# An attention and mixture-of-experts layer on one core: a prologue with real transposes, a stacked low-rank matmul, and V of batch 1 moved between the row maxima

## The chip, the cores and the metric

The kernel runs on one core of a Trainium2 chip. The metric is the device time of one execution in microseconds. The core has TensorE (PE; its weight loads are shown as PEld), VectorE (DVE), ScalarE (ACT), GpSimd (POOL) and SyncE (SP). Each runs its own list of instructions strictly in the order written, and they wait for one another by semaphores. SP and POOL also issue the DMAs here.

## The reference

The input x has 2 batches of 1024 tokens of 512 numbers, all float32. One post-norm layer is computed:

```python
def lora_linear(x, W, b, Bm, Am):                       # rank 16, SCALING = 0.5
    out = jnp.einsum('bld,od->blo', x, W) + b
    upd = jnp.einsum('blr,or->blo', jnp.einsum('bld,rd->blr', x, Bm), Am)
    return out + SCALING * upd
q, k, v = (_split(lora_linear(x, W, b, B, A)) for ...)  # 16 heads of 32
attn = jax.nn.softmax(jnp.einsum('bhqd,bhkd->bhqk', q, k) * SCALE, axis=-1)
out = jnp.einsum('bhqk,bhkd->bhqd', attn, v)            # back to (B, L, 512)
x = _layernorm(x + lora_linear(out, Wo, bo, Bo, Ao))
# 8 experts, hidden 704, top-1 routing with capacity 256, and a shared expert
x = _layernorm(x + moe(x, Wg, W1, W3, W2) + shared(x, sw1, sw3, sw2))
```

The low-rank update is folded into the weights: the kernel forms the transpose of W + 0.5 * Am Bm once for each of q, k, v and the output projection, and then needs a single matmul with it.

## The kernel before

**Two-part numbers.** Nearly every matmul runs in float32r (type FR). An operand is kept as a rounded high part, which ScalarE writes, and a low part (the rest), which VectorE writes by a subtraction. A product is three matmuls: high x high, high x low, low x high (`SPLIT`, `split3`, L712 to L718). So whatever comes out of TensorE into a PSUM bank and serves as an operand later goes through ScalarE and then through VectorE. There are 8 banks of 128 x 512.

**The prologue** is the part in front of the first attention half, and the only part that the change touches, but for three waits.

1. The four A matrices of the low-rank terms are transposed (L734) and copied by ScalarE, scaled by 0.5, to `lora_at` (L1114).
2. `weights(n)` makes one folded weight, in the order `W_ORDER` = v, q, k, output. Each has four chunks of 128 x 512. A chunk is a float32 matmul over 16 rows (the low-rank term, L747) and four float32 matmuls with the identity on top of it (the transpose of W, L750). Two banks alternate (`w_bank`). The parts of v stay in SBUF (`wv`); those of the others go through two staging buffers (`w_stage`) and by POOL's DMAs to DRAM (`wt_d`, L615), and a staging buffer is filled again when its store has landed (L1121, L1357).
3. x is loaded in 16 tiles of 128 tokens through four buffers (`xin`), transposed by TensorE (`turn_x`, L723) and split into `xT` (L1109, L1347).
4. `make_v` computes V for a token tile by 12 matmuls of 128 x 512 (L716), VectorE adds the bias (L1369) and POOL stores it to DRAM (`v_d`, L620), through two buffers `v_sb`.
5. TensorE's order of these is: weights(0) = v, x tiles 0 to 3, weights(1) = q, V 0 to 3, x 4 to 7, weights(2) = k, V 4 to 7, x 8 to 11, V 8 to 11, x 12 to 15, V 12 to 15.
6. Four projection units (12 matmuls each, L794) give k and q of batch 0 for the first four heads, with one chunk of the output weights behind each. ScalarE and VectorE split them into planes (L1145, L1388), and SP copies the planes into the stacked operands `Qs` and `Ks` (L420), 96 rows for each head.
7. The softmax needs the maximum of each score row. `PRO_USES` lists 44 score tiles (TensorE L806, VectorE's row maximum L1398) and one `mrow`, a transpose of the 16 columns of negated maxima (L810), stored by VectorE (L1402) and copied by SP to row 96 of `Qs` (L427). These go through three banks (`WORK`). `PRO_PLACE` puts three more projection units, for batch 1, as whole blocks behind score tiles 10, 18 and 26.
8. POOL, when all stores have landed and all of x is split, writes row 96 of both `Ks` with ones (L634).

Then attention runs in 16 halves (4 groups of 4 heads, 2 batches, 2 halves of 512 queries). A half computes transposed scores (L843), exponentials on ScalarE (L1172) into `prob`, and the product with V (L856). Between them, by the written orders `EVEN` and `ODD`, come the next halves' score tiles for the maxima and quarters of projection units. The first L843 marks the end of the prologue. The SBUF memory of `prob`, `Qs[1]` and `Ks[1]` is the same as that of the prologue's buffers, so ScalarE waits for all of the prologue's stores before its first exponential.

Of the kernel before, what the change touches and what calls it, by code (L numbers as in the profile page):

```python
# [51 lines left out]
W_ORDER = (2, 0, 1, 3)  # L52
# [70 lines left out]
PRO_USES = smax_uses(1) + [("mrow",)] + smax_uses(2, 0, EARLY[0])  # L123
PRO_PLACE = [10, 18, 26]
# [105 lines left out]
def emit(nc, ctx, x, W, bias, bo, Bm, Am, Wg, W1, W3, W2, sw1, sw3, sw2, out):  # L230
# [56 lines left out]
    xin = [stp(f"xin{i}", [P, D], F32) for i in range(4)]  # L287
    w_stage = [[stp(f"w_stage{i}{s}", [P, D], FR) for s in ("hi", "lo")] for i in range(2)]
# [82 lines left out]
    def _(sp):  # L371
# [14 lines left out]
        def load_x(i):  # L386
            for j in range(4):
                if i:
                    sp.wait_ge(sem("x_t"), 4 * i + j - 3)
                sp.dma_start(xin[j][:], x_rows[(4 * i + j) * P:(4 * i + j + 1) * P, :]).then_inc(sem(f"x_ld{j}"), 16)  # L390
# [63 lines left out]
        for i in range(2):  # L454
            for s in range(2):
                sp.wait_ge(sem(f"w_st{i}_{s}"), 16 * 6)

        def half(v):
            if v.proj and v.slot % 2 == 0:
# [4 lines left out]
                if not v.first:  # L464
                    sp.wait_ge(sem("pv_done"), used)
# [24 lines left out]
        def load_wo(v):  # L490

            sp.wait_ge(sem("st_full"), v.halves(HG * KC))
            for s in range(2):
                sp.dma_start(f32(wo[s][:]), wt_d[3, s]).then_inc(sem("wo_ld"), 16)
# [104 lines left out]
    def _(po):  # L599
# [9 lines left out]
        def store_w(n):  # L609
            m = W_ORDER[n]  # L610
            for dc in range(DC):
                k = (n - 1) * DC + dc
                po.wait_ge(sem("w_lo"), k + DC + 1)
                for s in range(2):
                    po.dma_start(wt_d[m, s][:, dc, :], f32(w_stage[k % 2][s][:])).then_inc(sem(f"w_st{k % 2}_{s}"), 16)  # L615

        def store_v(i):
            for t in range(4 * i, 4 * i + 4):
                po.wait_ge(sem("v_done"), t + 1)
                po.dma_start(v_d[t * P:(t + 1) * P, :], v_sb[t % 2][:]).then_inc(sem(f"v_st{t % 2}"), 16)  # L620

        store_w(1)
        store_v(0)
        store_w(2)
        for i in range(1, 4):
            store_v(i)
        store_w(3)
        for i in range(2):
            for s in range(2):
                po.wait_ge(sem(f"w_st{i}_{s}"), 16 * 6)  # L630
            po.wait_ge(sem(f"v_st{i}"), 16 * NT // 2)
        po.wait_ge(sem("x_lo"), NT)
        for i in range(2):
            po.memset(f32(Ks[i][96:97, :, :]), 1.0).then_inc(sem("ks_ones"), 1)  # L634
# [76 lines left out]
    def _(pe):  # L711
# [19 lines left out]
        pe.wait_ge(sem("lora_ld"), 16 * 8)  # L731
# [974 lines left out]
```

## Time and profile before

| | |
|---|---|
| median of 3 runs | 1193.78 us (1190.91, 1193.78, 1624.03) |
| the profiled execution | 1192.78 us |
| its span | 1191.2 us |
| mean granted TensorE clock | 0.954 |
| TensorE busy | 1126.8 us, 95% of the span, 5834 matmuls |
| VectorE busy | 722.0 us, 61% |
| ScalarE busy | 552.0 us, 46% |
| GpSimd busy | 482.7 us, 41% |
| DMA | 136.58 MB, 115 GB/s mean |

The span is cut by the program into pieces in which an engine is busy. A granted clock of 1.00 means TensorE's full 2.4 GHz, 0.50 means 1.2 GHz, and numbers between are means over a stretch. At the lower level every matmul takes twice as long and so TensorE shows as busy for twice as long; its busy share alone tells little. In the rows by stretch the columns are the stretch, its length, then busy time (and instructions) of PE, PEld, DVE, ACT and POOL, the granted clock, the share of the DMA engines and GB/s. A row of the chain of waits gives the start, the length, the engine and the line. In the rows in order of time a bracket gives the idle time of the engine in front of the group, and what ended it; "x11" means eleven instructions, and a float32 matmul over 128 rows or 16 rows shows as two. Where no bracket stands the engine hadn't been idle.

### The profile page before, as it was taken

To read this page: it belongs to the slowest core of one execution; us is meant where nothing else is said; L and a number is where in the kernel's file an instruction comes from. 1 tells how busy PE (TensorE), PEld (TensorE's weight loads), DVE (VectorE), ACT (ScalarE), POOL (GpSimd) and SP (SyncE) were. 2 spreads that over 40 slices of the span, in tenths; PEclk is the share of its full clock that TensorE was granted. 3 is DMA by queue.
4 is the path that set the end of the run, shared out by engine and by line. 5 is a ranking of instruction groups with operands and counts; after the bars stand their busy time and mean duration, and the time that the engine had idled before them with its cause. 6 is when DMAs were issued, how large, how long until landed. Compare 5 with 4: busy or idle time off the path is not lost.

```text
span 1191.2 us, 16459 instructions
## 1 busy us (share of the span) xinstructions
PE 1126.8 (95%) x5834; PEld 768.8 (65%) x5834; DVE 722.0 (61%) x1194; ACT 552.0 (46%) x960; POOL 482.7 (41%) x290
## 2 busy tenths in 40 slices
PE   7999689999999999999999979895999999999995
PEld 4687454656555564646543457674789999998774
DVE  1332476787877777777885468351356666664153
ACT  2211016565656656565666522331246666664125
POOL 0311207778584848587786731055000000002500
PEclk7999669999999999999999989897999999999997
DMA  4663415040332324140438253061147776765603
GB/s 155 221 207 110 120 28 134 25 98 30 76 94 63 81 58 120 37 107 21 99 85 230 60 173 106 18 207 23 53 116 220 203 226 198 233 192 119 100 1 141
DMA packets 151686, 136.58 MB, mean 115 GB/s; under 512 B 43121, under 2 KB 119153, under 8 KB 151360
## 3 DMA queue, kind: packets, MB, share of 16 engines
q1 hardware_dynamic: 143040, 113.45, 34.6%
q0 software_dynamic: 8576, 22.23, 6.5%
q8 instruction: 41, 0.67, 0.2%
q14 instruction: 29, 0.24, 0.1%
HBM read 79.72 MB, written 31.47 MB: 93 GB/s over the span
## 4 chain that ended last, share of the span: by engine, by line
PE 88%; DVE 5%; issue 2%; ACT 2%; DMA 1%; SPq 1%; POOL 0%; ACTq 0%; DVEq 0%
PE bank L716 27%; PE bank L972 11%; PE bank L843 11%; PE bank L806 11%; PE bank L856 10%; PE bank L794 8%; PE bank L868 4%; PE bank L750 2%; PE bank L723 2%; PE bank L747 2%; DVE mx L1398 1%; ACT rows L1314 1%; DVE rows L1530 1%; DMA at_in<-attn_d 0%; DVE xTlo L1347 0%
## 5 line engine op out<-in xcount | busy, mean ns | idle before, releaser
L1398 DVE TENSOR_REDUCE mx<-bank 128x1 f32<-128x512 f32 x512 | 322.6, 680 | 114.6 <-PE bank L806 112.5
L1172 ACT ACTIVATE prob<-bank 128x512 f32<-128x512 f32 x512 | 289.7, 597 | 202.4 <-PE bank L843 189.2
L646 POOL TENSOR_TENSOR psum<-psum,prob 128x1024 f32<-128x1024 f32 x122 | 286.8, 2395 | 0.0
L843 PE MATMUL bank<-Qs,Ks 97*128 97x512 f32 x512 | 208.7, 424 | 1.0 <-ACT prob L1172 0.9
L806 PE MATMUL bank<-Ks,Qs 96*128 96x512 f32 x512 | 196.1, 431 | 11.7 <-DMA Qs<-plane_qhi 7.3
L843 PEld LDWEIGHTS bank<-Qs,Ks 97*128 97x128 f32 x512 | 96.0, 189 | 111.5 <-ACT prob L1172 74.4
L646 POOL TENSOR_TENSOR psum<-prob,prob 128x1024 f32<-128x1024 f32 x32 | 75.8, 2388 | 176.7 <-PE bank L868 133.2
L806 PEld LDWEIGHTS bank<-Ks,Qs 96*128 96x128 f32 x512 | 100.2, 197 | 60.7 <-DVE mx L1398 24.2
L856 PE MATMUL bank<-prob,V 128*32 128x512 f32 x1024 | 131.4, 601 | 0.0
L695 POOL DMA_DIRECT2D oe_d<-oe_sb x16 | 8.7, 547 | 256.4 <-ACT oe_sb L1294 255.4
L1239 ACT ACTIVATE sa<-bank 128x256 f32<-128x256 f32 (+1 forms) x72 | 32.7, 455 | 157.5 <-PE bank L716 120.4
L1516 DVE TENSOR_TENSOR sa<-bank,sa 128x256 f32<-128x256 f32 (+1 forms) x72 | 37.0, 514 | 109.0 <-ACT sa L1239 86.1
L794 PE MATMUL bank<-xThi,Wsl 128*128 128x512 f32 x256 | 101.6, 419 | 0.0
L1440 DVE RECIPROCAL bank<-bank 128x128 f32<-128x128 f32 x64 | 60.2, 951 | 14.8 <-PE bank L868 14.8
L794 PEld LDWEIGHTS bank<-xThi,Wsl 128*128 128x128 f32 x256 | 51.7, 202 | 12.5
L856 PEld LDWEIGHTS bank<-prob,V 128*32 128x32 f32 x1024 | 24.0, 108 | 51.3 <-issue 35.0
L794 PE MATMUL bank<-xTlo,Wsl 128*128 128x512 f32 x128 | 53.0, 414 | 0.0
L972 PE MATMUL bank<-w2hi,hid0hi 128*128 128x512 f32 x96 | 39.8, 415 | 9.0 <-issue 8.7
L972 PE MATMUL bank<-w2hi,hid1hi 128*128 128x512 f32 (+1 forms) x96 | 39.5, 412 | 2.8 <-DVE hid1lo L1518 2.8
L1509 DVE TENSOR_TENSOR w2lo<-raw,w2hi 128x512 fp32r<-128x512 f32 (+1 forms) x60 | 41.0, 685 | 1.9 <-ACT w2hi L1232 1.8
L681 POOL DMA_INDIRECT xd_d<-rows,sidx x16 | 17.0, 1060 | 57.1 <-DVE sidx L1580 52.6
L972 PE MATMUL bank<-w2hi,hid0lo 128*128 128x512 f32 x96 | 38.6, 402 | 0.8 <-issue 0.8
(213 smaller groups left out, 2147.5 us busy)
## 6 DMA issues: line engine op xcount, KB each, us to landing
raw<-in_L_ffn_W_dram SPq DMA_DIRECT2D x120, 256.0 KB
Ks<-plane_khi SPq DMA_DIRECT2D x64, 128.0 KB, 2.3
Qs<-plane_qhi SPq DMA_DIRECT2D x64, 128.0 KB, 2.3
raw<-in_L_ffn_sw_dram SPq DMA_DIRECT2D x30, 256.0 KB
xin<-in_L_attn_x_dram SPq DMA_DIRECT2D x16, 256.0 KB, 4.2
v_d<-v_sb POOLq DMA_DIRECT2D x16, 256.0 KB, 2.3
Wsl<-wt_d SPq DMA_DIRECT2D x16, 256.0 KB, 4.3
Ks<-plane_klo SPq DMA_DIRECT2D x32, 128.0 KB, 2.3
```

Of the source, the lines that this page charges most:

```text
L646: po.tensor_tensor(psum[:, pr], (prob[0] if kc == 1 else psum)[:, pr], prob[kc % RING][:, pr], ALU.add).then_inc(sem("sum_done"), 1)
L716: mm = nc.tensor.matmul(dst, lhs(a, dc), rhs(b, dc), start=dc == 0 and k == 0, stop=dc == DC - 1 and k == 2)
L794: mm = nc.tensor.matmul(pj, Wsl[:, m, a, dc, :], xT[p][:, dc, cols], start=dc == 0 and k == 0, stop=dc == DC - 1 and k == 2)
L806: mm = nc.tensor.matmul(dst, Qs[b][0:96, hh, q0:q0 + P], Ks[b][0:96, hh, part * 512:part * 512 + 512], start=True, stop=True)
L843: nc.tensor.matmul(score_at(v, i), Ks[v.b][0:97, hh, kc * P:(kc + 1) * P], Qs[v.b][0:97, hh, v.hf * HALF:(v.hf + 1) * HALF], start=True, s ...
L856: mm = nc.tensor.matmul(ov[hh * HD:(hh + 1) * HD, :], V[b][:, kc % KC, hh * HD:(hh + 1) * HD], prob[kc % RING][:, hh, :], start=kc == 0, s ...
L868: mm = nc.tensor.matmul(dn[hh * HD:(hh + 1) * HD, :], ones32[:], part[:, hh, :], start=summed[n] == 1, stop=summed[n] == KC - SUMS[n] + 1)
L972: mm = nc.tensor.matmul(bank[4 + i], hid[c % 2][a][p0:P, i * P:(i + 1) * P], w2[p][p0:P, c, :], start=c == 0 and k == 0, stop=c == FC - 1 ...
L1172: ACTV(prob[kc % RING][:, hh, :], score_at(v, i), ACT.Exp, scale=SCALE).then_inc(sem("exp_done"), 1)
L1398: ins = RED(mx[(hf + ahead) % 2][:, 4 * hh + qt, part:part + 1], src, AX.X, ALU.max)
L1440: nc.vector.reciprocal(part, part).then_inc(sem("rden"), 1)
L1509: TT(w2[1][p0:P, c], raw2[c % 2][p0:P, :], f32(w2[0][p0:P, c]), ALU.subtract).then_inc(sem("conv2"), 1)
```

## The change

- `W_ORDER` becomes q, k, v, output.
- A weight chunk is four transposes in TensorE's transpose form and then one float32r matmul over 80 rows. Its operands are `bs` and `as_`: B is loaded five times, one copy for each 16 rows (`load_b`), ScalarE rounds all 80 rows and VectorE puts the low part into rows 32 to 47; A's high part is copied by ScalarE to rows 0 and 32, and VectorE puts its low part into row 64 on; the rows between are zeroed by POOL first. The matmul so adds the three products of the split at once.
- x has eight buffers instead of four. Its last eight tiles are turned behind the four projection units.
- V is computed for tiles 0 to 3 behind the three weights, for 4 to 7 between the first four projection units, and for batch 1 (8 to 15) by quarters in a written order `PRO_ORDER`: `m` is a score tile, `r` the mrow, `v` a quarter of V, `a` VectorE's addition and POOL's store for it, `p` a quarter of a projection unit, `q` its split, `w` a chunk of the output weights, `s` its split and store.
- `mrow` comes after 36 score tiles instead of 32.
- The second `Ks` row of ones is written at the end, the first at the start. Some waits for stores move to where the data is first used.

```diff
-W_ORDER = (2, 0, 1, 3)
+W_ORDER = (0, 1, 2, 3)
+RSTACK = 80
...
-PRO_USES = smax_uses(1) + [("mrow",)] + smax_uses(2, 0, EARLY[0])
-PRO_PLACE = [10, 18, 26]
+PRO_USES = smax_uses(1) + smax_uses(2, 0, 4) + [("mrow",)] + smax_uses(2, 4, EARLY[0])
+PRO_ORDER = ("vvvv a vm vm vm vm a vm vm vm vm a vm vm vm vm a wm pm pm pm pm s vm "
+             "vmq vm vm a wm vm s vm vm vm a pm pm pm pm wm vm sq vm vm vm a wm r "
+             "s vm vm vm vm a pm pm pm pm q")
...
+    fresh = Arena(nc, small_at - V_BYTES * 2, small_at)
+    xin += [fresh(f"xin{i}", [P, D], F32) for i in range(4, 8)]
...
+    def staged(n, dc):
+
+        return (n if n < 2 else n - 1) * DC + dc
...
         for m in range(4):
-            sp.dma_start(lora_b[32 * m:32 * m + RANK, :], Bm[m]).then_inc(sem("lora_ld"), 16)
             sp.dma_start(lora_a[:, m], Am[m].rearrange("(c p) r -> p c r", p=P)).then_inc(sem("lora_ld"), 16)
+
+        def load_b(m):
+
+            for r in range(0, RSTACK, RANK):
+                sp.dma_start(lora_b[r:r + RANK, m], Bm[m]).then_inc(sem("b_ld_first" if m == 0 else "b_ld"), 16)
...
         load_w(0)
+        load_b(0)
         load_x(0)
+        for m in range(1, 4):
+            load_b(m)
         load_w(1)
-        sp.dma_start(bv_bc[:], bias[2].rearrange("(o d) -> o d", o=1).to_broadcast([P, D])).then_inc(sem("bv_ld"), 16)
         load_x(1)
         load_w(2)
+        sp.dma_start(bv_bc[:], bias[2].rearrange("(o d) -> o d", o=1).to_broadcast([P, D])).then_inc(sem("bv_ld"), 16)
+        load_w(3)
         load_x(2)
         load_x(3)
-        load_w(3)
...
-        stack_unit(0, 3, 4)
+        stack_unit(0, 2, 4)
         for i in range(2):
-            sp.wait_ge(sem(f"v_st{i}"), 16 * NT // 2)
+            sp.wait_ge(sem(f"v_st{i}"), 16 * NT // 4)
+        sp.wait_ge(sem("x_t"), NT)
         load_v(0, 0)
...
+        po.wait_ge(sem("const"), 2)
+        po.memset(f32(as_[0:RSTACK]), 0.0).then_inc(sem("as_zero"), 1)
+        po.wait_ge(sem("as_zero"), 1)
+        po.memset(f32(Ks[0][96:97, :, :]), 1.0).then_inc(sem("ks_ones"), 1)
+        for n in range(2):
             for dc in range(DC):
...
+                store_w(n, dc)
+        for t in range(2 * DC):
+            store_v(t)
+        t, dc = 2 * DC, 0
+        for w in "".join(PRO_ORDER.split()):
+            if w == "a":
+                store_v(t)
+                t += 1
+            elif w == "s":
+                store_w(3, dc)
+                dc += 1
         for i in range(2):
             for s in range(2):
                 po.wait_ge(sem(f"w_st{i}_{s}"), 16 * 6)
...
+        po.memset(f32(Ks[1][96:97, :, :]), 1.0).then_inc(sem("ks_ones"), 1)
...
-            pe.wait_ge(sem("a_ev"), n + 1)
+            pe.wait_ge(sem("a_lo"), n + 1)
+            pe.wait_ge(sem("b_lo"), 1 if n == 0 else 2)
             pe.wait_ge(sem(f"w_ld{n % 2}"), 16 * (n // 2 + 1))
...
-                nc.tensor.matmul(dst, lora_b[32 * m:32 * m + RANK, dc * P:(dc + 1) * P],
-                                 lora_at[32 * m:32 * m + RANK, :], start=True, stop=False)
                 for oc in range(DC):
-                    mm = nc.tensor.matmul(dst[:, oc * P:(oc + 1) * P], w_raw[n % 2][:, oc, dc * P:(dc + 1) * P],
-                                          ident[:], start=False, stop=oc == DC - 1)
+                    nc.tensor.matmul(dst[:, oc * P:(oc + 1) * P], w_raw[n % 2][:, oc, dc * P:(dc + 1) * P],
+                                     ident[:], start=oc == 0, stop=False, is_transpose=True)
+                mm = nc.tensor.matmul(dst, bs[0:RSTACK, m, dc * P:(dc + 1) * P], as_[0:RSTACK, m, :],
+                                      start=False, stop=True)
                 mm.then_inc(sem("w_mm"), 1)
...
+        pe.wait_ge(sem("a_lo"), 4)
         weights(0)
-        pe.wait_ge(sem("a_ev"), 4)
         turn_x(0)
         weights(1)
-        make_v(0)
         turn_x(1)
         weights(2)
-        make_v(1)
-        for i in (2, 3):
-            turn_x(i)
-            make_v(i)
+        for t in range(4):
+            make_v(t)
...
-        pe.wait_ge(sem("x_lo"), NT)
-
         for n, (m, ph) in enumerate(PRO_PROJ[:4]):
             project_unit(m, ph, 0, range(DC), n or None, 48)
-            weights(3, n, n + 1)
...
+            make_v(4 + n)
+        turn_x(2)
+        turn_x(3)
+        pe.wait_ge(sem("x_lo"), NT)
...
+        def split_a(n):
+
+            m = W_ORDER[n]
             ac.wait_ge(sem("a_t"), n + 1)
-            ACTV(lora_at[32 * m:32 * m + RANK, :], bank[n][0:RANK, :], ACT.Copy, scale=LORA).then_inc(sem("a_ev"), 1)
+            for r in (0, 32):
+                ACTV(as_[r:r + RANK, m], bank[n][0:RANK, :], ACT.Copy, scale=LORA).then_inc(sem("a_ev"), 1)
+
+        ac.wait_ge(sem("as_zero"), 1)
+        split_a(0)
+        ac.wait_ge(sem("b_ld_first"), 16 * 5)
+        ACTV(bs[0:RSTACK, 0], lora_b[0:RSTACK, 0], ACT.Identity).then_inc(sem("b_hi"), 1)
+        for n in range(1, 4):
+            split_a(n)
+        ac.wait_ge(sem("b_ld"), 16 * 15)
+        ACTV(bs[0:RSTACK, 1:4], lora_b[0:RSTACK, 1:4], ACT.Identity).then_inc(sem("b_hi"), 1)
...
+                if n != 2 and at >= 2:
+                    ac.wait_ge(sem(f"w_st{at % 2}_0"), 16 * (at // 2))
+                ACTV(wv[0][:, dc, :] if n == 2 else w_stage[at % 2][0][:], w_bank(k),
                      ACT.Identity).then_inc(sem("w_hi"), 1)
```

In the written order TensorE, ScalarE, VectorE and POOL each walk through `PRO_ORDER` and take the letters that are theirs. VectorE's part of the split of A and B:

```diff
+        def split_a(n):
+
+            m = W_ORDER[n]
+            ve.wait_ge(sem("a_ev"), 2 * n + 2)
+            nc.vector.scalar_tensor_tensor(out=as_[64:64 + RANK, m], in0=bank[n][0:RANK, :], scalar=LORA,
+                                           in1=f32(as_[0:RANK, m]), op0=ALU.mult, op1=ALU.subtract).then_inc(sem("a_lo"), 1)
+
+        def split_b(k, ms):
+
+            ve.wait_ge(sem("b_hi"), k + 1)
+            TT(bs[32:32 + RANK, ms], lora_b[32:32 + RANK, ms], f32(bs[32:32 + RANK, ms]),
+               ALU.subtract).then_inc(sem("b_lo"), 1)
```

## Rows read from the trace of the kernel before

**Rows 1.** The page's part 4, shares of the chain of waits by engine.
```profile
PE 88%; DVE 5%; issue 2%; ACT 2%; DMA 1%; SPq 1%; POOL 0%; ACTq 0%; DVEq 0%
```

**Rows 2.** Busy time by stretch: us; each engine's busy time; granted clock, DMA.
```profile
0.00:36.00 36.00, 28.77 (x113) 18.07 (x114) 6.82 (x10) 9.49 (x15) 3.27 (x12) 0.81 0.57 181
118.00:126.00 8.00, 0.73 (x7) 0.57 (x5) 0.69 (x1) 0.60 (x1) 1.35 (x3) 0.79 0.90 262
126.00:161.00 35.00, 29.93 (x68) 19.02 (x68) 21.56 (x35) 2.06 (x3) 6.67 (x2) 0.65 0.21 51
168.50:180.00 11.50, 10.93 (x38) 8.21 (x36) 9.20 (x15) 6.45 (x12) 3.87 (x2) 0.77 0.11 25
180.00:200.00 20.00, 20.00 (x112) 8.79 (x116) 13.68 (x24) 13.12 (x24) 19.62 (x9) 1.00 0.49 112
```

**Rows 3.** Chain of waits in order of time: start us, us, what.
```profile
6.57 3.56 PE bank L734 x16
27.56 1.05 PE bank L747 x2
28.61 1.09 PE bank L750 x8
36.12 11.21 PE bank L716 x48
47.33 1.75 PE bank L723 x16
60.41 11.58 PE bank L716 x48
98.87 2.81 PE bank L794 x12
168.52 0.43 PE bank L843
174.00 0.23 PE bank L843
```

**Rows 4.** SyncE's issues in order of time: start us, us, what.
```profile
3.90 0.50 SPq L378 DMA_DIRECT2D lora_b<-in_L_attn_Bo_dram  x1
4.44 0.42 SPq L379 DMA_DIRECT2D lora_a<-in_L_attn_Ao_dram  x1
```

**Rows 5.** DMA issues of the first 195 us: size, median us to landing.
```profile
w_raw<-in_L_attn_Wv_dram SPq DMA_DIRECT2D x1, 1024.0 KB, 5.7
lora_b<-in_L_attn_Bo_dram SPq DMA_DIRECT2D x1, 32.0 KB, 2.2
wt_d<-w_stage0hi POOLq DMA_DIRECT2D x6, 256.0 KB, 2.7
wt_d<-w_stage1hi POOLq DMA_DIRECT2D x6, 256.0 KB, 3.6
```

**Rows 6.** ScalarE in order of time, in brackets the idle time before.
```profile
10.15 0.58 ACT L1114 ACTIVATE lora_at<-bank 16x512 f32<-16x512 f32 x1 [0.24 <-PE bank L734]
37.12 0.60 ACT L1122 ACTIVATE w_stage0hi<-bank 128x512 fp32r<-128x512 f32 x1 [4.65 <-DMA wt_d<-w_stage0hi]
```

**Rows 7.** VectorE in order of time.
```profile
30.36 0.69 DVE L1358 TENSOR_TENSOR w_stage0lo<-bank,w_stage0hi 128x512 fp32r<-128x512 f32 x1 [1.32 <-ACT w_stage0hi L1122]
86.65 2.47 DVE L1347 TENSOR_TENSOR xTlo<-bank,xThi 128x512 fp32r<-128x512 f32 x4
117.24 0.75 DVE L1388 SCALAR_TENSOR_TENSOR plane_qlo<-bank,bcol,plane_qhi 128x512 fp32r<-128x512 f32 x1 [2.19 <-ACT plane_qhi L1145]
126.69 6.67 DVE L1398 TENSOR_REDUCE mx<-bank 128x1 f32<-128x512 f32 x11 [6.72 <-PE bank L806]
```

**Rows 8.** GpSimd in order of time.
```profile
31.38 0.77 POOL L615 DMA_DIRECT2D wt_d<-w_stage0hi  x1 [29.70 <-DVE w_stage0lo L1358]
125.72 6.95 POOL L634 MEMSET Ks<- 1x4096 f32 x2 [4.38 <-DMA wt_d<-w_stage1lo]
```

**Rows 9.** TensorE in order of time, after the gap at 118 us.
```profile
125.89 6.53 PE L806 MATMUL bank<-Ks,Qs 96*128 96x512 f32 x11 [7.27 <-DMA Qs<-plane_qhi]
```

More of the change, by code:

```diff
@@ L463, in half @@
                 c, used = value(v.g * P + (v.h // 4 * P + v.b * P)), value(v.halves(KC))
-                if not v.first:
+                if v.first:
+                    for i in range(2):
+                        sp.wait_ge(sem(f"v_st{i}"), 16 * NT // 2)
+                else:
                     sp.wait_ge(sem("pv_done"), used)
@@ L492, in load_wo @@
             sp.wait_ge(sem("st_full"), v.halves(HG * KC))
+            for i in range(2):
+                for s in range(2):
+                    sp.wait_ge(sem(f"w_st{i}_{s}"), 16 * 6)
             for s in range(2):
@@ L630, in _ @@
                 po.wait_ge(sem(f"w_st{i}_{s}"), 16 * 6)
[L631 to L634, printed above, removed]
+        po.memset(f32(Ks[1][96:97, :, :]), 1.0).then_inc(sem("ks_ones"), 1)
+        po.wait_ge(sem("ks_ones"), 2)
         def sums(n):
@@ L730, in _ @@
         pe.wait_ge(sem("const"), 2)
[L731 removed]
+        pe.wait_ge(sem("lora_ld"), 16 * 4)
         for n, m in enumerate(W_ORDER):
@@ L767, in make_v @@
                     pe.wait_ge(sem("v_done"), t - 1)
-                split3(bank[6 + t % 2], lambda a, dc: xT[a][:, dc, t * P:(t + 1) * P],
-                       lambda p, dc: wv[p][:, dc, :]).then_inc(sem("v_mm"), 1)
+            for dc in quarters:
+                for k, (a, p) in enumerate(SPLIT):
+                    mm = nc.tensor.matmul(bank[6 + t % 2], xT[a][:, dc, t * P:(t + 1) * P], wv[p][:, dc, :],
+                                          start=dc == 0 and k == 0, stop=dc == DC - 1 and k == 2)
+            if DC - 1 in quarters:
+                mm.then_inc(sem("v_mm"), 1)
+        pe.wait_ge(sem("a_lo"), 4)
         weights(0)
-        pe.wait_ge(sem("a_ev"), 4)
         turn_x(0)
         weights(1)
-        make_v(0)
         turn_x(1)
         weights(2)
-        make_v(1)
-        for i in (2, 3):
-            turn_x(i)
-            make_v(i)
+        for t in range(4):
+            make_v(t)
         def project_unit(m, ph, b, quarters, n, ld_need):
@@ L1149, in _ @@
             plane_hi(m, ph, n + 1, 48, None)
-            weights(3, n, n + 1)
+        turned_x(2)
+        turned_x(3)
+        i, dc = 4, 0
+        for w in "".join(PRO_ORDER.split()):
+            if w == "q":
+                plane_hi(*PRO_PROJ[i], i + 1, 48, 96)
+                i += 1
+            elif w == "s":
+                weights(3, dc, dc + 1)
+                dc += 1
         for i in range(2):
@@ L1362, in turned_x, with make_v @@
                 turned(i, j, bank[j], "x_hi", "x_lo")
-        def make_v(i):
-            for t in range(4 * i, 4 * i + 4):
-                ve.wait_ge(sem("v_mm"), t + 1)
-                if t >= 2:
-                    ve.wait_ge(sem(f"v_st{t % 2}"), 16 * (t // 2))
-                TT(v_sb[t % 2][:], bank[6 + t % 2], bv_bc[:], ALU.add).then_inc(sem("v_done"), 1)
+        def make_v(t):
+            ve.wait_ge(sem("v_mm"), t + 1)
+            if t >= 2:
+                ve.wait_ge(sem(f"v_st{t % 2}"), 16 * (t // 2))
+            TT(v_sb[t % 2][:], bank[6 + t % 2], bv_bc[:], ALU.add).then_inc(sem("v_done"), 1)
         weights(0)
@@ L1373, in _ @@
         weights(1)
-        ve.wait_ge(sem("bv_ld"), 16)
-        make_v(0)
         turned_x(1)
         weights(2)
-        make_v(1)
-        for i in (2, 3):
-            turned_x(i)
-            make_v(i)
+        ve.wait_ge(sem("bv_ld"), 16)
+        for t in range(4):
+            make_v(t)
         def plane_lo(m, ph, n):
@@ L1409, in _ @@
             plane_lo(m, ph, n + 1)
-            weights(3, n, n + 1)
-        for n, kind in enumerate(PRO_USES):
-            use(kind, n, n + 1, 1, None)
-            if n - 1 in PRO_PLACE:
-                i = 4 + PRO_PLACE.index(n - 1)
+            make_v(4 + n)
+        turned_x(2)
+        turned_x(3)
+        n, i, t, dc = 0, 4, 2 * DC, 0
+        for w in "".join(PRO_ORDER.split()):
+            if w in "mr":
+                use(PRO_USES[n], n, n + 1, 1, None)
+                n += 1
+            elif w == "a":
+                make_v(t)
+                t += 1
+            elif w == "q":
                 plane_lo(*PRO_PROJ[i], i + 1)
+                i += 1
+            elif w == "s":
+                weights(3, dc, dc + 1)
+                dc += 1
         def half(v):
```

115 lines of the change are left out of this document (58 added, 57 removed).

## The prediction

> **What bounds the kernel now.** I read the page's chain of waits first: TensorE carries 88% of it, VectorE 5% [rows 1]. Only the prologue is touched, so the busy time by stretch comes next [rows 2]. From 0 to 36 us TensorE is busy for 28.8 us at a granted clock of 0.81. From 118 to 126 us it does 0.73 us of work, and from 126 to 161 us it shows 29.9 us busy in 35, but at a clock of 0.65, mostly the lower of the two levels (1.2 of 2.4 GHz). That stretch holds 32 score tiles for the row maxima and three projection units of 12 matmuls, 15.9 us of work at the full-clock price below; VectorE and hand-overs set its length. The chain in order of time [rows 3] gives the unit prices, and the moment by which I measure: the first score of attention starts at 168.52 us. All code after it is the same but for a few waits.
>
> **The prices at full clock** [rows 3]. A V tile is 12 matmuls, 11.21 / 4 = 2.80 us; a projection unit 2.81; a 128x512 matmul 0.234. Four real transposes are 1.75 / 4 = 0.44. A weight chunk today is a 16-row float32 matmul of 1.05 and four float32 matmuls with the identity, 1.09 / 2 = 0.54 for one chunk; the two rows each cover one chunk, as their records (x2 and x8) show, so the chunk is 1.05 + 1.09 = 2.14.
> The new chunk is four transposes and one float32r matmul of 80 rows. No row shows that matmul: between 0.234 (float32r, 128 rows) and 1.05 (float32, 16 rows) I take 0.234, the row of its own type. The transposes lie between 0.44 (the same form on x) and 1.09; I take 0.44. A chunk is then 0.67, and 16 chunks save 23.5 us of TensorE at full clock. That isn't yet time saved, since in the new order they wait for others.
>
> **Step 1, the start.** SP issues four loads of A, then the first weight, then five of B, four of x, fifteen of B, the second weight. At 0.46 for an A load and 0.50 to 0.54 for a B load [rows 4] the A loads are issued by 2.8 us and landed 2 us later, where today the last is issued at 4.44 and TensorE starts at 6.57 [rows 3, 4]. So the 3.56 us of A transposes run from 4.5 to 8.1. The five first B loads are issued by 5.9 but stand behind the 1 MB weight, issued at 2.8, which takes 5.7 us to land [rows 5]: about 8.7. The fifteen others are issued from 8.1 to 15.8 and land 2.2 us later [rows 5]: 17.5 at the latest with some queueing behind x.
> ScalarE splits A in eight copies of 0.58 [rows 6] and converts B. Its order is A(0), B(0) after 8.7, A(1) to A(3) to 13.0, then the wait for all fifteen B loads, then a conversion of 1536 columns (3 x 0.60 = 1.8; at the least 0.6), to 19.1. Only then does it take the first weight bank. TensorE waits for the last A split, 13.8 against 10.78 today, does two chunks and stops, as there are two banks. VectorE splits B in 3 x 0.62 [rows 7] = 1.8 us, so the first two low parts are ready at 21.5 and 22.1 us. POOL's zero fill of A before that is half the width of one 3.5 us fill [rows 8], done by 3.5 us; at the price of both fills it would be done at 8.6 and delay ScalarE by little.
>
> **Step 2, the ring of stores.** q and k are now converted one behind the other, eight chunks through two staging buffers; nothing but x's four tiles stands between. A round is ScalarE 0.60 [rows 6], VectorE 0.69 [rows 7], 0.33 to reach POOL and the store's landing: 2.7 us for the first buffer, 3.6 for the second [rows 5], but 5.7 where loads ran beside it (store issued at 31.38, ScalarE released at 37.12 [rows 6, 8]). Today this wait is under V work. Now the second weight, x and the third weight (3 MB) are in flight until about 30 us, so the first round gets 5.5; the next two get 2.7 and 3.8. High parts then start at 19.1, 27.3, 32.1, 36.4, the last (chunk 7) at 39.6. x's second four tiles follow (ScalarE 40.2 to 42.3), then v's weights without stores: two chunks at once, two more a round later, the last low part at 46.8. V begins at **46.9**. With all rounds at 5.7 it would be 54; all clean, 43.
>
> **Step 3, V tiles 0 to 3.** 11.2 us. TensorE has done some 12 us of work in the 33 us before, so I let it start at half clock. After the gap at 118 it ran at half for long [rows 2, 9]; after a stretch of full occupation it was back within about 5 us (from 168.52 to 174.00 matmuls go from 0.43 to 0.23 [rows 3]). Five us at half cost 2.6: V ends at 60.7. The clock cost lies between 0 and 11.2.
> The loads of Wsl and bcol (SP waits for the last k store, landed at about 46) are six issues and a landing, ready before that even at 8 us for a landing.
>
> **Step 4, four projection units between V tiles 4 to 7.** 8 x 2.80 = 22.4, to 83.1. The last unit is ready at 80.3, and 1.5 us later (ScalarE 0.70, VectorE 0.75 [rows 7]) SP may stack q. Today the first score tile came 125.89 - 117.99 = 7.9 us after that [rows 7, 9]: now 89.7. **Step 5, x tiles 8 to 15**: VectorE bounds them, 0.7 + 8 x 0.62 [rows 7] + hand-overs, to 88.9. So the 7.3 us wait for the stacks is covered by this and the next four quarters of V.
>
> **Step 6, the written order.** 32 quarters of V (22.4), 12 of projections (8.4), 44 score tiles (10.3), 4 chunks (2.7) and one small transpose: 43.9 us of TensorE. VectorE has 44 x 0.61 [rows 7] + 8 x 0.69 + 4 x 0.69 + 3 x 0.75 = 37.4, so TensorE bounds it, if no hand-over cuts in; per group "vm vm vm vm a" it is 3.74 against 3.1. Half clock for 5 us after the transposes of step 5 costs 2.5. The end is 88.9 + 43.9 + 2.5 = **135.3**. What could be late: the row maxima's transfer (r stands 7.5 us of TensorE work before the end; SP needs 4 x 0.54 for the issues and 2.2 to land) and the last V store (its tile is ready some 4 us before the end; 0.69 + 0.33 + 2.3), on which ScalarE's first exponential waits. I add 0.2: first score at 135.5, 33.0 earlier. POOL's second fill (3.5 us [rows 8]) now lies between the last store and its first sum, which wants six exponentials, 3.6 us; the k stacks of batch 1 wait for the last unit, now at the end, but are wanted behind the q stacks, which come with the first half's own unit.
>
> **Step 7, entry into attention.** From 168.5 to 180 us 38 matmuls took 10.9 us at clock 0.77 [rows 2]; at 0.234 they are 8.9. TensorE now comes in warm: 2.0 more.
>
> **The sum**: 33.0 + 2.0 = 35.0 us. The profiled execution took 1192.78 us (span 1191.2) and gives 1157.8; the median of three runs, 1193.78, is 0.1% above it, so I say **1158** for the median.
>
> **Clock and transposes.** The x transposes ran at full clock between V tiles (1.75 us [rows 3]); no row shows transposes alone for longer. The Trainium skill, "TensorE: Matmul & The Clock Gate", Part 4, says transpose mode doesn't count as busy for the gate. This speaks against the change: it turns the filler before V into such work, and by that rule the two cold starts of steps 3 and 6 are certain; without it the sum would be the second rival's.
>
> **The rivals.**
> 1. As summed: 1150 to 1166. Chance 0.56.
> 2. The clock holds through the transposes, both cold starts vanish: 5.1 less, 1153. For it: from 27.6 to 36 us short weight work ran at full clock [rows 3]. Against: the long gap. 0.12.
> 3. The ring: every round at the congested 5.7 or more, V at 54 to 58: 1165 to 1169, 1172 if the B loads are late as well. For it: two weights and x are in flight at that time, and the one store seen beside such loads took 5.7. 0.13.
> 4. The written order has hand-over gaps, and TensorE runs at half clock in a third of it, as it did at 0.65 with 85% busy [rows 2]: 43.9 / 3 = 14.6 more, 1172. Against: in steady attention the same mix of quarters and score tiles runs at full clock, as from 180 us [rows 2]. 0.14.
> 5. The transposes cost two passes (0.65 more a chunk): hidden in steps 1 and 2, 2.6 in step 6: 1161. 0.02.
> 6. Slower: the clock stays at 1.2 GHz from the first V tile to the first score. TensorE's work there is 11.2 + 22.4 + 43.9 = 77.5 us, doubled, less the 5.1 counted: 72.4, so 1230. It is slower than before once over 40 of these 77.5 us of work run at half clock. Against: TensorE is full there, and under V the clock came back soon (the 48 matmuls from 60.41 took 11.58, against 11.21 [rows 3]). 0.03.
>
> **The numbers.** About 2% (24 us) is what a measurement here tells from no change; faster means below 1169.9. Faster: 0.56 + 0.12 + 0.02 + most of 3 + a third of 4 = 0.83; same 0.14; slower 0.03. The range, 1148 to 1174, takes in the clean ring and warm clock at the low end (1158 - 4 - 5) and rivals 3 and 4 at the high one.
>
> **What would show it.** First score near 135 us. First high weight part on ScalarE at 19 us, not before the last B load. ScalarE waits of about 5, 3 and 3 us for the store of a staging buffer. V's first matmul at 47 us at 0.43. The first score tile without a wait for stacks. From 89 us TensorE over 95% busy at clock 1.0. The stretch from first score to end shorter by 2 us, no more. It would be wrong if ScalarE's or VectorE's fixed order made TensorE wait within the written order, or if the stores cost more than 6 us a round.

## The result and the profile after

| | before | after |
|---|---|---|
| median | 1192.35 us (4 runs) | 1161.70 us (4 runs, 1161.27 to 1163.08) |
| the profiled execution, its span | 1192.78, 1191.2 us | 1163.08, 1161.5 us |
| first score of attention | 168.52 us | 137.16 us |
| mean granted clock | 0.954 | 0.969 |

One of the four executions of before took 1624.03 us and is left out of what follows; the other three have a median of 1190.91 us. The ratio is 0.975 (95% interval 0.972 to 0.979): 29.2 us faster by the medians, 29.7 by the profiled executions. The forecast was 1158, in a range from 1148 to 1174. A repeat of both on another chip gave 0.975 (0.972 to 0.979) again.

Lines of the page's part 1 and part 4, which answer to the table of before and to [rows 1]:

```profile
PE 1086.5 (94%) x5754; PEld 752.0 (65%) x5754; DVE 728.3 (63%) x1200; ACT 556.1 (48%) x966; POOL 484.7 (42%) x291
...
PE 85%; DVE 6%; SPq 3%; DMA 2%; issue 2%; ACT 2%; POOL 0%; ACTq 0%; DVEq 0%
```

TensorE shows 40.3 us less busy time (1126.8 before) and its share of the chain falls from 88% to 85%. SP with 3% and the DMAs with 2% stand in the chain now. In front of V the chain has 12 us of SP's issues and 17 of DMAs; the next largest part, 13.5 us of SP and 5.5 of a DMA, leads to the load of `bcol` at 308 us, shown below. By stretch (the columns are those of [rows 2]):

```profile
15.00:49.00 34.00, 19.40 (x92) 15.88 (x92) 14.81 (x22) 12.35 (x21) 8.87 (x16) 0.83 0.91 303
49.00:63.00 14.00, 13.90 (x49) 11.11 (x50) 2.12 (x4) 0.00 (x0) 1.63 (x3) 0.80 0.51 166
97.00:137.20 40.20, 40.20 (x183) 32.41 (x182) 36.18 (x58) 3.75 (x7) 9.89 (x17) 1.00 0.34 121
```

From 15 to 49 us TensorE is busy for 19.4 of 34 us. From 97 to 137.2 us, the written order, it is busy for all of 40.2 us at clock 1.00, with VectorE at 36.2 beside it; the answering stretch of before had 29.93 of 35 at 0.65. The chain in order of time (start, length, what; answers to [rows 3]):

```profile
16.22 1.50 ACT bs L1171
...
21.30 4.41 DMA wt_d<-w_stage0lo
...
27.33 5.06 DMA wt_d<-w_stage0lo
...
35.13 5.91 DMA wt_d<-w_stage1lo
...
49.10 13.97 PE bank L799 x48
63.07 2.79 PE bank L824 x12
...
86.54 3.96 DVE xTlo L1409 x7
...
91.47 5.31 PE bank L799 x15
```

These are the stages of the forecast: the last B conversion at 16.22, three stores of low parts that the chain passes through (4.41, 5.06 and 5.91 us to landing), V from 49.10 (13.97 us, cold), the first projection unit at 63.07, the x tiles at VectorE's pace from 86.54, and V tile 8 from 91.47, whose first 15 matmuls take 5.31 instead of 3.5. ScalarE in order of time shows the ring of stores (answers to [rows 6]):

```profile
17.61 0.58 ACT L1179 ACTIVATE w_stage0hi<-bank 128x512 fp32r<-128x512 f32 x1
...
24.54 0.60 ACT L1179 ACTIVATE w_stage0hi<-bank 128x512 fp32r<-128x512 f32 x1 [5.72 <-DMA wt_d<-w_stage0hi]
27.22 0.60 ACT L1179 ACTIVATE w_stage1hi<-bank 128x512 fp32r<-128x512 f32 x1 [2.08 <-DMA wt_d<-w_stage1hi]
...
31.65 0.60 ACT L1179 ACTIVATE w_stage0hi<-bank 128x512 fp32r<-128x512 f32 x1 [1.88 <-DMA wt_d<-w_stage0hi]
32.98 0.60 ACT L1179 ACTIVATE w_stage1hi<-bank 128x512 fp32r<-128x512 f32 x1 [0.74 <-DMA wt_d<-w_stage1hi]
36.24 0.60 ACT L1179 ACTIVATE w_stage0hi<-bank 128x512 fp32r<-128x512 f32 x1 [2.66 <-DMA wt_d<-w_stage0hi]
39.51 0.60 ACT L1179 ACTIVATE w_stage1hi<-bank 128x512 fp32r<-128x512 f32 x1 [2.67 <-DMA wt_d<-w_stage1hi]
```

Each high part with a bracket waited for the store of the buffer that it fills. TensorE at the first score and at one place further on (answers to [rows 9]):

```profile
137.16 0.40 PE L886 MATMUL bank<-Qs,Ks 97*128 97x512 f32 x1
...
147.44 0.50 PE L886 MATMUL bank<-Qs,Ks 97*128 97x512 f32 x1 [0.57 <-ACT prob L1234]
```

```profile
308.13 0.50 PE L824 MATMUL bank<-xThi,Wsl 128*128 128x512 f32 x1 [1.59 <-DMA bcol<-in_L_attn_bk_dram]
```

The same place in j, the second trace of the changed kernel:

```profile
307.08 0.50 PE L824 MATMUL bank<-xThi,Wsl 128*128 128x512 f32 x1 [0.82 <-DMA bcol<-in_L_attn_bk_dram]
```

### The profile page after: what moved, and what is told of

The parts are those of the page before. It is cut to its first block, busy times and chain, and to the rows that moved or that the text cites. A ratio compares the mean times of both kernels' runs of the same rounds, so it can differ in the third digit from the quotient of the medians.

```text
span 1161.5 us, 16337 instructions
## 1 busy us (share of the span) xinstructions
PE 1086.5 (94%) x5754; PEld 752.0 (65%) x5754; DVE 728.3 (63%) x1200; ACT 556.1 (48%) x966; POOL 484.7 (42%) x291
## 4 chain that ended last, share of the span: by engine, by line
PE 85%; DVE 6%; SPq 3%; DMA 2%; issue 2%; ACT 2%; POOL 0%; ACTq 0%; DVEq 0%
PE bank L744 24%; PE bank L1017 12%; PE bank L886 11%; PE bank L899 10%; PE bank L836 10%; PE bank L824 8%; PE bank L799 4%; PE bank L911 4%; PE bank L751 1%; DVE xTlo L1409 1%; DVE mx L1475 1%; DMA wt_d<-w_stage0lo 1%; SPq L438 1%; SPq L394 1%; ACT rows L1376 1%
## 5 line engine op out<-in xcount | busy, mean ns | idle before, releaser
L836 PE MATMUL bank<-Ks,Qs 96*128 96x512 f32 x512 | 189.4, 406 | 1.3 <-DVE mx L1475 1.1
L836 PEld LDWEIGHTS bank<-Ks,Qs 96*128 96x128 f32 x512 | 96.4, 189 | 41.3 <-DVE mx L1475 11.9
L824 PE MATMUL bank<-xThi,Wsl 128*128 128x512 f32 x256 | 97.8, 397 | 1.6 <-DMA bcol<-in_L_attn_bk_dram 1.6
L824 PEld LDWEIGHTS bank<-xThi,Wsl 128*128 128x128 f32 x256 | 48.3, 189 | 13.6 <-DMA bcol<-in_L_attn_bk_dram 2.0
L824 PE MATMUL bank<-xTlo,Wsl 128*128 128x512 f32 x128 | 50.4, 394 | 0.0
L1017 PE MATMUL bank<-w2hi,hid0hi 128*128 128x512 f32 x96 | 39.8, 415 | 8.4 <-issue 8.1
L1017 PE MATMUL bank<-w2lo,hid0hi 128*128 128x512 f32 x96 | 38.8, 404 | 0.0
```

The lines of the kernel that those rows point to most:

```text
L824: mm = nc.tensor.matmul(pj, Wsl[:, m, a, dc, :], xT[p][:, dc, cols], start=dc == 0 and k == 0, stop=dc == DC - 1 and k == 2)
L836: mm = nc.tensor.matmul(dst, Qs[b][0:96, hh, q0:q0 + P], Ks[b][0:96, hh, part * 512:part * 512 + 512], start=True, stop=True)
L1017: mm = nc.tensor.matmul(bank[4 + i], hid[c % 2][a][p0:P, i * P:(i + 1) * P], w2[p][p0:P, c, :], start=c == 0 and k == 0, stop=c == FC - 1 ...
```

## The experiments

All are variants of the changed kernel or, for b, of the kernel before. Times are medians; the ratios to the kernel before on the same chip stand with their intervals. a to d ran on one chip, g, h, e and f on a second, j, k, l and i on a third. Where a first exponential is compared, it comes from one trace of each kernel.

### a: the new order with the old chunk

```diff
-                for oc in range(DC):
-                    nc.tensor.matmul(..., start=oc == 0, stop=False, is_transpose=True)
-                mm = nc.tensor.matmul(dst, bs[0:RSTACK, m, ...], as_[0:RSTACK, m, :], start=False, stop=True)
+                nc.tensor.matmul(dst, lora_b[32 * m:32 * m + RANK, ...], lora_at[32 * m:32 * m + RANK, :], start=True, stop=False)
+                for oc in range(DC):
+                    mm = nc.tensor.matmul(..., ident[:], start=False, stop=oc == DC - 1)
```

(with the loads and the split of A and B as before the change)

> The new order with the old weight chunk (a 16-row float32 matmul and four float32 matmuls with the identity, B loaded once). Theory 'order': the weights now stand in front of V, where the ring of stores and the split of B set the pace, so the dearer chunk is partly hidden and its start is earlier (no split of B); it costs the 4 x 1.47 us in the written order and some us before V: 4 to 10 us more than the changed kernel, 1166 to 1172 us. Rival 'chunk': every microsecond of TensorE counts, 16 x 1.47 = 23.5 us more, 1185 us.

Measured: 1172.56 us, 0.986 (0.982 to 0.991). The chain of waits:

```profile
11.32 2.04 PE bank L764 x2
13.37 2.00 PE bank L767 x8
...
29.57 7.30 DMA wt_d<-w_stage1lo
...
50.51 2.01 PE bank L767 x8
...
57.94 4.21 PE bank L787 x9
```

```profile
105.50:152.00 46.50, 46.50 (x204) 35.04 (x203) 36.95 (x59) 3.85 (x7) 10.20 (x17) 1.00 0.30 108
```

It is nearer to theory 'order' than to the rival, just above its range; in the traces the first exponential comes 14.7 us after the changed kernel's (152.4 for 137.7), more than that theory allows. The first weight is made from 11.32 to 27.4 us with TensorE busy all along and every row at 2.00 us, where the same rows took 1.05 and 1.09 in [rows 3]. That is the price of the half clock, though the profile gives a granted clock of 1.00 for this stretch; from 46.5 to 56.5 us it gives 0.50 with the same 2.00 us. V starts at 57.94 instead of 49.10: but for one store of 7.30 us, here the chunk isn't hidden but is itself the pace. The written order takes 46.5 instead of 40.2 us, and 4 x 1.47 = 5.9 was forecast.

### b: the new chunk in the old order

```diff
 # before.py: chunk, loads of B, split_a, split_b and the zero fill as in the change
 W_ORDER = (2, 0, 1, 3)   # and all stages in the old order
```

> The old order with the new weight chunk alone. Theory: in the old order V stands between the weights and hides the ring, so the cheaper chunk is paid in full except at the start, where the split of B makes it 5 us later: q -4, k with its cold stretch -9, output weights -6: about 19 us less than the kernel before, 1173 us. Rival 'additive': it is worth only what the order leaves over, 31 us minus the 25 that filling the gaps would bring, about 6 us, 1186 us.

Measured: 1180.42 us, 0.992 (0.990 to 0.995), between theory and rival. Two places in the chain show where the expected 19 us stay:

```profile
29.93 8.28 DMA wt_d<-w_stage1hi
...
40.36 8.40 PE bank L728 x24
...
93.19 2.82 PE bank L807 x12
...
96.75 0.76 DVE plane_klo L1430
...
97.65 3.05 PE bank L807 x12
...
102.34 3.03 PE bank L807 x12
```

First, VectorE stands at the low part of a q chunk until its store has landed (8.28 us), and V's bias addition is queued behind it, so V tiles wait: V tile 3 is done at 48.8 us, against 47.3 before. Second, between the projection units there is now 0.67 us of chunk where a unit's split takes 1.5 us, and TensorE waits: the units start 4.46 and 4.69 us apart (93.19, 97.65, 102.34), against 4.93 to 4.95 before (98.87, 103.82, 108.75), so 0.2 to 0.5 is saved where the chunk is 1.47 cheaper. The first exponential comes at 158.1 us, 10.9 earlier. Only 6.2 of that is there at the first score tile (119.74 for 125.89). The other 4.7 arise in the row maxima, whose code is that of before:

```profile
119.70:157.60 37.90, 32.05 (x82) 18.97 (x83) 28.30 (x48) 2.06 (x3) 5.52 (x2) 0.77 0.26 62
```

Before, this stretch took 42.6 us at a clock of 0.62. Why the clock was higher in b isn't shown, so these 4.7 us can't be put down to the chunk.

### c: V of batch 1 ahead of the row maxima

```diff
-PRO_ORDER = ("vvvv a vm vm vm vm a vm vm vm vm a ..."
+PRO_ORDER = ("vvvv a vvvv a ... (eight tiles) m m m m m m m m m ..."   # then the same order without v and a
```

> The changed kernel with V of batch 1 in eight whole blocks ahead of the row maxima, and everything else of the written order as it is. Theory 'fill': the blocks cost 22.4 us of TensorE, the row maxima then run at VectorE's pace, 44 x 0.61 + 4 x 0.69 + 3 x 0.75 = 32 us or more, with TensorE falling to half clock: first score about 146 to 149 instead of 137.2, total 1171 to 1174 us. Rival: TensorE's work is the same, so it stays within 2 us of the changed kernel, 1162 us.

Measured: 1179.34 us, 0.991 (0.988 to 0.994), 17.6 us above the changed kernel's median on another chip and 19.0 later at the first exponential (156.7 for 137.7); the rival is out, and theory 'fill' named too small a size.

```profile
117.00:157.00 40.00, 35.41 (x103) 23.42 (x102) 31.91 (x54) 4.54 (x8) 8.35 (x10) 0.74 0.16 60
```

From the first score tile to the first score of attention the row maxima take 39.8 us without any V in them. In the changed kernel the same work *with* 28 quarters of V, 19.6 us of TensorE's time, takes 40.5. VectorE works for 31.9 of the 40 us; in the rest, TensorE ran at a mean clock of 0.74 and projection quarters at half clock held up score tiles. V between the maxima is all but free, and with it the clock is 1.00. How much of this is the free time of TensorE and how much the clock isn't separated: at full clock the maxima alone could be up to 8 us shorter (40 less VectorE's 31.9, an estimate), and V would then cost that much.

### d, k: four staging buffers

```diff
+    w_stage += [[ring(f"w_stage{i}{s}", [P, D], FR) for s in ("hi", "lo")] for i in (2, 3)]   # in the planes' memory
-                if n != 2 and at >= 2:
-                    ac.wait_ge(sem(f"w_st{at % 2}_0"), 16 * (at // 2))
+                if n != 2 and at >= 4:
+                    ac.wait_ge(sem(f"w_st{buf(at)}"), stored(at))
```

> The changed kernel with four staging buffers for the weights of q and k instead of two. Theory 'ring': the three waits of ScalarE and VectorE for stores (5.7, 1.9, 2.7 us and more) vanish, V starts at about 41 us instead of 49, and the total falls by 7 to 9 us, to about 1154 us. Rival: the loads of the next weights and x, which run at the same time, set the pace; V starts less than 3 us earlier, 1159 to 1162 us.

> The changed kernel with four staging buffers, on the same chip as its base. Theory 'ring': 7 to 9 us below the changed kernel, all of it before V's first matmul. Rival, that the loads set the pace: under 3 us.

Measured: d 1153.48 us, 0.971 (0.966 to 0.976); k, on another chip and beside the changed kernel, 1155.47 us, 0.969 (0.965 to 0.972), against 1161.81. That is 6.3 us by the medians of one chip (8.2 for d, across chips) and 7.0 at the first exponential (130.4 for 137.4). ScalarE of k, and two rows of its chain:

```profile
21.86 0.60 ACT L1185 ACTIVATE w_stage2hi<-bank 128x512 fp32r<-128x512 f32 x1 [2.68 <-PE bank L785]
...
25.95 0.60 ACT L1185 ACTIVATE w_stage0hi<-bank 128x512 fp32r<-128x512 f32 x1
27.61 0.60 ACT L1185 ACTIVATE w_stage1hi<-bank 128x512 fp32r<-128x512 f32 x1 [1.06 <-DMA wt_d<-w_stage1lo]
32.17 0.60 ACT L1185 ACTIVATE w_stage2hi<-bank 128x512 fp32r<-128x512 f32 x1 [3.97 <-DMA wt_d<-w_stage2lo]
35.68 0.60 ACT L1185 ACTIVATE w_stage3hi<-bank 128x512 fp32r<-128x512 f32 x1 [2.90 <-DMA wt_d<-w_stage3lo]
```

```profile
25.29 10.31 DMA wt_d<-w_stage3lo
...
85.67 3.77 PE bank L805 x15
```

V starts at 44.3 us in k, 5.1 earlier than in j, and at 44.7 in d, not at 41: both between theory and rival. The first four chunks and the fifth have no wait for a store now, but the last three still do, one of them for a store that took 10.31 us to land, with the loads of two weights and x beside it. So the ring is a cause, and the loads are the next.

The theory wanted the whole gain ahead of V, and 1.9 of the 7.0 us aren't there. V takes 12.99 us for 13.37 in j, and the 15 matmuls from V tile 8 on take 3.77 for 5.31, although the block of x tiles in front of them is the same in both (in k and in the changed kernel 34 instructions, 4.23 us busy in 6.1). So that block doesn't settle the clock that follows it: without g's change it came out warm in d and k, and cold in the changed kernel's two traces and in a, c, e and h.

### g: x tiles 8 to 15 by pairs between V and the projections

```diff
             make_v(4 + n)
+            turn_x(None, (8 + 2 * n, 9 + 2 * n))
-        turn_x(2)
-        turn_x(3)
```

> The changed kernel with x tiles 8 to 15 turned by pairs behind each of V tiles 4 to 7, not as one block behind them. Theory: the block takes 6.0 us at VectorE's pace and leaves TensorE idle for 1.7, with a cold start behind it (5.31 us for 15 matmuls that cost 3.5); spread out they cost 8 x 0.44 = 3.5 us of TensorE and no cold start: 4 us less than the changed kernel, 1157 to 1158.5 us. Rival: the first row maxima then wait for the stacks of q (landed about 91 us), and the gain is under 1.5 us.

Measured: 1141.40 us, 0.974 (0.971 to 0.978) on a chip where the kernel before takes 1172.83. The ratio doesn't tell it from the changed kernel's 0.975. The trace does, up to the first score:

```profile
85.26 2.80 PE bank L799 x12
88.06 0.45 PE bank L751 x4
...
90.50 3.76 PE bank L799 x15
```

V tile 8 starts at 90.50 instead of 91.47 and isn't cold (15 matmuls in 3.76 us); the first exponential comes at 135.2 instead of 137.7. So 2.5 us, and not 4: the last pair still goes through ScalarE and VectorE before V tile 8 may start. Of the 2.5 us 1.5 are the clock, and d and k had that without this change; all four kernels with pairs (g, f, l, i) come out warm, so that pairs keep the clock is likely and not shown.

### h: fillers before V

```diff
         turn_x(1)
-        weights(2)
+        weights(2, 0, 1)
+        filler(8)          # matmuls of 128x512 into a bank that V writes later
+        weights(2, 1, 2)
+        filler(6)
+        weights(2, 2, 4)
+        filler(3)
```

> The changed kernel with 17 matmuls of 128x512 whose result nobody reads, put into TensorE's idle time between the chunks of v's weights, just before V. Theory 'cold start': V tiles 0 to 3 take 13.97 us instead of 11.2 because TensorE comes out of idle stretches at half clock; with the fillers it comes in at full clock, V takes 11.2 to 11.5 and the time falls by about 2.3 us to 1159.4 us, though the fillers can delay v's chunks by up to 1 us. Rival: the clock of that stretch isn't set by the idle time just before it; V stays near 14 us and the total the same or up to 2 us more.

Measured: 1140.51 us, 0.972 (0.969 to 0.976), on the same chip as g.

```profile
38.00:49.00 11.00, 8.72 (x48) 6.63 (x47) 5.66 (x10) 4.84 (x9) 2.14 (x4) 1.00 1.00 345
```

```profile
44.95 0.63 PE bank L777 x4
...
47.91 11.47 PE bank L799 x48
```

The clock is 1.00 in front of V, the two late chunks take 0.88 (0.63 and 0.25) and 0.68 us instead of 1.55 and 1.28, V starts at 47.91 instead of 49.10, and its 48 matmuls take 11.47 instead of 13.97. First exponential: 134.0, 3.7 us earlier. Theory 'cold start' stands: the clock in front of V sets V's time. l, which has no fillers but also made its last chunk at full clock, takes the same 11.47 us. The total again lies inside the interval of the changed kernel's ratio.

### e, f, l, i: the start, and all together

```diff
 # e: four buffers, and on ScalarE and VectorE behind weights(0) instead of ahead of it:
+        weights(0)
         for n in range(1, 4):
             split_a(n)
         ac.wait_ge(sem("b_ld"), 16 * 15)
-        weights(0)
 # f and l: e with g's x tiles;  i: f with load_x(2), load_x(3), load_w(3) behind load_slot(0)
```

> Four staging buffers, and the split of A(1) to A(3) and the conversion of the other fifteen B loads moved behind the first weight on ScalarE and VectorE. Theory: the first high part of a weight comes at about 12.5 us instead of 18, and V starts at about 40 us instead of 44.7: 4 to 5 us less than with four buffers alone (1153.5), 1149 us. Rival: the loads and stores that run at the same time set the pace there (a store took 8 us to land with four buffers): under 1.5 us less.

> The former and the x tiles by pairs between V and projections: the two gains add, about 1145 us if both theories hold, 1149 us if only one does, 1153 us if neither.

> Four staging buffers, the other splits of A and B behind the first weight, x tiles 8 to 15 by pairs between V and projections, on the same chip as its base. V started at 39 us in the earlier trace instead of 49, but the first projection unit waited until 52.7 for Wsl and bcol, whose loads stand behind the last store (10 us to land). About 12 us below the changed kernel.

> The former with the loads of x tiles 8 to 15 and of the output weights (3 MB) issued behind Wsl and bcol instead of ahead of the last stores. Theory: the last k store and the load of Wsl no longer share the queues with 3 MB that nobody needs before 58 us; the store lands in 4 to 5 us instead of 10, the first projection unit follows V tile 3 without a wait, 1.5 to 3 us less than the former. Rival: the x tiles now come late for their place between V and projections, and TensorE waits for them at 58 us: the same or up to 3 us more.

Measured: e 1133.79 us, 0.966 (0.962 to 0.971); f 1131.30, 0.965 (0.961 to 0.969), both on the second chip. l, the same kernel as f, 1151.46, 0.966 (0.962 to 0.969); i 1147.80, 0.963 (0.960 to 0.967), both on the third. e's first high part is at 13.08 us, near the 12.5 expected, but its V starts at 41.9, not 40, and the gain is gone by the first exponential: 130.5 us, for 131.0 in d and 130.4 in k. V took 14.01 us and V tile 8 started cold (5.31), where d had 13.24 and 3.76. So in the traces the rival's number holds; by the ratios e is lower, but the intervals overlap, and that it is faster than four buffers alone isn't shown. f's first exponential is at 125.1, and its ratio is that of the text's middle case, 1149 us, in which one theory holds. f's chain and l's:

```profile
20.15 12.14 DMA wt_d<-w_stage3lo
...
34.52 10.25 DMA wt_d<-w_stage3lo
...
46.22 6.45 DMA bcol<-in_L_attn_bk_dram
...
52.72 3.06 PE bank L830 x12
```

```profile
18.41 17.25 DMA w_raw<-in_L_attn_Wv_dram
...
42.03 11.47 PE bank L805 x48
```

In f two stores take 12.14 and 10.25 us and the first projection waits for `bcol`, behind them. In l the projection doesn't wait; there V waits for v's weights, whose load of 1 MB is issued at 18.41 and takes 17.25 us; its last chunk is at full clock and V takes 11.47. Either way the start is bound by transfers now: W, x and the stores together. i moved 3 MB of loads away and its median is 3.7 us lower, but the intervals overlap and its profiled execution, first exponential at 126.9 against l's 125.6, doesn't show the forecast mechanism. That i is better than l isn't shown. Both are faster than the changed kernel on the same chip, by 10.4 and 14.0 us; about 12 was expected for l.

### j: the changed kernel again

> The changed kernel itself, beside the next three on one chip, as their base: 0.975 of the kernel before by all theories, whatever the chip's own level is. If only the prologue differs between the two, the first score comes about 31 us earlier and the rest of the two traces takes the same time within 2 us.

Measured: 1161.81 us, 0.975 (0.972 to 0.979). First exponential at 137.4 us, 31.6 earlier than in the trace of before; behind it the spans are 1024.8 and 1022.2 us. The 2.6 us by which the rest is longer are a little more than the 2 expected; most of them arise in the output projections (from the first to the last tile 64.9 us against 62.4), a stretch that took between 61.8 and 65.9 us in the kernels shown here, all with the same code.

## Why the prediction was right, and where it was off

The direction, the place and nearly the size were right: 31.36 us at the first score where 33.0 were forecast. That it came so near is in part luck, as errors of 1.5 and 3.7 us in steps 1 and 2 went opposite ways. By its steps:

| step | forecast | measured |
|---|---|---|
| 1, first high part | 19.1 us | 17.61 |
| 2, V starts | 46.9 | 49.10 |
| 3, V 0 to 3 | 13.8 long | 13.97 |
| 4, projections and V 4 to 7 | 22.4 | 22.4 |
| 5, x tiles 8 to 15 | 5.8 | 6.0 |
| 6, written order | 46.4 | 45.7 |
| first score | 135.5 | 137.16 |
| 7, entry into attention | 2.0 gained | 1.1 gained |
| the rest | 0 | 2.8 lost |

**Step 1** was 1.5 us too long: a load of B took 0.42 us to issue, not 0.50 to 0.54, and the last of them landed at 16.2 us instead of 17.5.

**Step 2** was mis-sized, 31.5 us from the first high part to V instead of 27.8, and in part for a reason that the text had in hand. It let a round end with the landing of the high part's store (2.7 to 5.5 us). VectorE writes the low part, whose store is issued 0.53 to 0.77 us later and landed 4.41, 5.06 and 5.91 us after its issue; the chain runs through those three. Up to the last high part of k this costs 1.4 us (21.9 for 20.5; the part itself came at 39.51, for 39.6 forecast, as step 1 was early). The last low part of k waits for its buffer's low store, 1.0 more, and is done at 41.82. From there to V it is 7.3 us for 6.0, as v's last two chunks run at half clock. h shows the clock's share: 1.2 us before V and 2.5 in V.

**Steps 3 and 6** counted two cold starts, 2.6 and 2.5 us. Both came, the second smaller: V took 13.97 (h: 11.47 when warm), and V tile 8's first 15 matmuls 5.31, which is 1.8 more than at full clock (g: 3.76). So rival 2, the clock holding through the transposes, didn't occur in the changed kernel's traces. That it can is shown by d and k, where V tile 8 came out of the same block of x tiles warm (3.76 and 3.77 us). The Trainium skill's rule that transposes don't count as busy ("TensorE: Matmul & The Clock Gate", Part 4) gives a cold start behind them every time; six traces here agree and those two don't. Nor does a run here tell transposes from idle time: TensorE stood still for 15 of the 34 us before V too.

**Step 6**'s claim that TensorE bounds the order was right to 0.7 us, and these are the smaller cold start. c shows what was behind it: half clock in parts of the order, as in rival 4, is what happens when V is *not* there.

**Step 7** gave 1.1 instead of 2.0 (10.28 us from the first score to the first matmul that waited for an exponential, for 11.42 before): warm, TensorE waits 0.76 us for a row maximum, VectorE's pace.

**The rest** was put at nothing and cost 2.8. Of it 1.9 is one load of `bcol` that came late at 308 us. TensorE waits 1.59 us for it, 0.82 in j and 0.5 to 0.9 in c, e, f, g, h, i and l; it doesn't wait in the trace of before or in a, b, d and k. So nine of the twelve traces with the new order have the wait and neither of the two with the old one: it looks like an effect of the change, but how it comes about isn't shown. In the changed kernel the issue of one `Qs` copy took SP 2.05 us (at 297.71) just ahead of it, 0.59 in the trace of before. Another 1.3 us lie in the output projections (63.7 us for 62.4), whose length varies between executions of the same code.

**How the gain divides.** The order alone (a) gives 17.5 us, the chunk alone (b) 9.6, both together 28.3 on the third chip and 29.2 in the first comparison: close to their sum. Neither half behaves as expected, though. In a the dearer chunk holds V back by 8.8 us, as TensorE makes 13 of the 24 rows of chunks in front of V at 2.00 us; in b a cheaper chunk uncovers the splits that it used to hide, and 4.7 us of b's gain in its trace lie in a stretch that it doesn't change. That the two numbers add up to the whole may be chance. Of the 23.5 us of TensorE's time that the chunk saves, 5.9 to 6.3 are saved in the written order and 8.8 before V.

## What to carry to other kernels

Look for a place between the work of another engine: 19.6 us of TensorE between VectorE's row maxima cost 0.7 us here, where the same work in a block cost nearly its full length (18.2 us more from V tile 8 to the first score), and the clock was 1.00 with it. When an order puts all transfers into one stretch, follow each buffer round, the later of two stores included, and count what else is in flight; four buffers instead of two brought V forward by another 5.1 us here. Check a gain at its place as well as in the total: in e 2.8 us in front of V were gone again by the first score, and in b 4.7 us came from a stretch with the old code, with another clock both times. Before making a small operation cheaper, look at what it covers: between the projection units, 1.47 us less of TensorE gave 0.2 to 0.5.

## What was not expected of the hardware

- A store of 256 KB landed in 2.3 us (the median of V's sixteen) and in 2.6 us at the least for weights' high parts, but took 4.4 to 5.9 us beside weight and x loads, 8.3 in b, and 10.3 to 12.1 with more of them in flight; a 1 MB load took 5.7 us at the start and 17.25 in l. The Trainium skill ("DMA: Bandwidth & Descriptors", Anatomy of one DMA) has about 2.0 us and the bytes at 436 GB/s for one that GpSimd issues, which makes 2.6 us for 256 KB (an estimate from its figures): the lone stores are at or below that, and the loaded ones 1.7 to 4.7 times as long.
- TensorE without a gap didn't always have its full clock: in a the float32 passes of the first weight ran back to back for 16 us at 2.00 us a row, and again from 46.5 us, at a granted clock of 0.50; in the trace of before the clock is 0.50 from 15 to 25 us with TensorE busy for all of the 10 us. From V tile 4 on a tile took 2.79 to 2.80 us again in a and in the changed kernel.
- The granted clock of a trace's first microseconds isn't to be relied on: it reads 1.00 from 11.3 to 27.4 us in a, and from 15 to 25 us in the changed kernel, where the four transposes of a chunk take 1.1 us instead of 0.6 in the rows in order of time. Only the rows' own lengths tell the level there, and the 0.83 of 15 to 49 us above is too high for it.
- The second chip ran the kernel before 17 to 18 us faster (1172.83 against 1190 to 1191). In its four traces (e, f, g, h) the time from the first exponential to the end is 1001.7 to 1005.2 us, in the ten others 1020.3 to 1024.8, and up to the output projections there is no difference. In the ten TensorE stands still for 11.5 to 14.0 us in all between 700 and 900 us, most of it at once in the expert stage's start, waiting for nothing that the profile shows, and then runs at half clock; in the four it doesn't. What it waits for wasn't tried.
